# A decoder layer stack on one core: the memory layer's softmax sums move to TensorE, its division to VectorE behind the values, and the normalisations' epsilon to GpSimd

## The reference, cut to what matters

```python
x = x + L0_attn(_layernorm(x))                       # attention
x = x + L0_xattn(_layernorm(x), ctx, mask0)          # linear cross attention
x = x + L0_ffn(_layernorm(x))                        # gated feed-forward
x = x + L1_attn(_layernorm(x))                       # feature attention
x = x + L1_xattn(_layernorm(x), ctx, mask1)          # memory layer
x = x + L1_ffn(_layernorm(x))                        # ternary feed-forward

def _L1_xattn_ref(hidden_states, memory_tokens, memory_mask, norm_w, wq, wk, wv, wo, wg):
    x = rmsnorm(hidden_states, norm_w)
    q, k, v = x @ wq.T, memory_tokens @ wk.T, memory_tokens @ wv.T   # 16 heads of 16
    attn = jnp.einsum('blhd,bmhd->bhlm', q, k) * scale
    attn = jnp.where(memory_mask[:, None, None, :], attn, -jnp.inf)
    attn = jnp.nan_to_num(jax.nn.softmax(attn, axis=-1), nan=0.0)
    out = jnp.einsum('bhlm,bmhd->blhd', attn, v).reshape(B, L, C) @ wo.T
    return jax.nn.sigmoid(x @ wg.T) * out
```

## Time and profile before

| | |
|---|---|
| median of 3 runs | 916.41 us (916.15 to 917.59) |
| the profiled execution | 914.14 us, span 912.3 us |
| mean granted TensorE clock | 0.994 |
| busy: TensorE, VectorE, ScalarE, GpSimd | 93%, 78%, 59%, 41% of the span |

### The profile page before, as it was taken

One profiled execution on the slowest core, in us unless ns is written; L12 is line 12 of the kernel. 1 busy time (PEld: TensorE's weight loads), 2 busy tenths in 40 slices (PEclk: granted clock), 3 DMA queues, 4 the chain that ended last, 5 costly groups with the idle time before them and its releaser, 6 DMA issues. The chain is left out here.

```text
span 912.3 us, 18715 instructions
## 1 busy us (share of the span) xinstructions
PE 848.8 (93%) x6868; PEld 630.7 (69%) x6868; DVE 707.6 (78%) x1749; ACT 539.0 (59%) x1285; POOL 373.0 (41%) x358
## 2 busy tenths in 40 slices
PE   6888998999999999999999998999978889999786
PEld 3555766777777777777777776887855578777554
DVE  5647967887788788877887774997688779886985
ACT  1655576665666566656665655464566864546676
POOL 6014555545555555545554644052242031522410
PEclk9999999999999999999999999999999999999999
DMA  9133131101110111011100000000000010000001
GB/s 279 40 83 93 22 94 36 31 6 35 35 26 8 35 35 35 0 35 35 35 0 11 1 1 2 2 1 1 1 1 1 1 47 1 1 1 1 1 1 47
DMA packets 34723, 25.56 MB, mean 28 GB/s; under 512 B 9492, under 2 KB 31596, under 8 KB 34668
## 3 DMA queue, kind: packets, MB, share of 16 engines
q1 hardware_dynamic: 34380, 24.56, 10.1%
q10 hardware_dynamic: 288, 0.26, 0.1%
HBM read 22.65 MB, written 2.17 MB: 27 GB/s over the span
## 5 line engine op out<-in xcount | busy, mean ns | idle before, releaser
L502 POOL CAST exp_hi<-exp_scores 128x1024 f16<-128x1024 f32 x64 | 67.0, 1047 | 199.4 <-ACT exp_scores L628 199.4
L504 POOL TENSOR_TENSOR exp_lo<-exp_scores,exp_hi 128x1024 f16<-128x1024 f32 x64 | 140.7, 2198 | 5.1
L628 ACT ACTIVATE exp_scores<-banks,exp_bias,unscale 128x256 f32<-128x256 f32 x256 | 141.0, 560 | 2.1
L75 PE MATMUL banks<-value_out_hi,xn_t_hi 128*128 128x256 f16 x512 | 139.6, 273 | 0.8 <-DVE X L961 0.5
L76 PE MATMUL banks<-value_out_lo,xn_t_hi 128*128 128x256 f16 x512 | 139.5, 273 | 0.0
L77 PE MATMUL banks<-value_out_hi,xn_t_lo 128*128 128x256 f16 x512 | 139.5, 273 | 0.0
L1119 PE MATMUL banks<-qk 128*128 128x256 f32 x512 | 121.6, 380 | 8.5 <-ACT exp_scores L628 8.4
L1119 PEld LDWEIGHTS banks<-qk 128*128 128x128 f32 x512 | 96.6, 190 | 29.4 <-issue 8.7
L961 DVE SCALAR_TENSOR_TENSOR X<-banks,colsum,X 128x256 f32<-128x256 f32 x256 | 106.2, 478 | 12.8 <-DVE colsum L952 11.4
L573 ACT ACTIVATE qk<-banks 128x512 f32<-128x512 f32 x128 | 75.8, 601 | 58.9 <-PE banks L77 58.9
L75 PE MATMUL banks<-xn_t_hi,head_weights_hi 128*128 128x512 f16 x256 | 96.9, 378 | 2.4 <-ACT qk L573 1.6
(11 more groups left out here) (254 smaller groups left out, 1962.4 us busy)
## 6 DMA issues: line engine op xcount, KB each, us to landing
head_weights<-in_wqkv_d SPq DMA_DIRECT2D x32, 128.0 KB, 3.8
weight_absmax_rows<-across_partitions SPq DMA_DIRECT2D x15, 256.0 KB, 4.2
X<-in_x_d SPq DMA_DIRECT2D x4, 512.0 KB, 7.6
head_weights<-in_wqkvt_d SPq DMA_DIRECT2D x16, 128.0 KB, 3.5
head_weights<-in_w_o_d SPq DMA_DIRECT2D x16, 128.0 KB, 3.5
out<-X SPq DMA_DIRECT2D x8, 256.0 KB, 2.1
ternary_then_kv_and_rows<-in_c_fc_d SPq DMA_DIRECT2D x1, 1024.0 KB, 5.0
ternary_then_kv_and_rows<-in_c_proj_d SPq DMA_DIRECT2D x1, 1024.0 KB, 8.0
```

The costliest lines, as they stand in the source:

```text
L75: nc.tensor.matmul(out, lhs[0], rhs[0], start=first, stop=False)
L502: nc.gpsimd.tensor_copy(probh[:, s1_.par], prob[:, s1_.par]).then_inc(exph_ready, 1)
L504: nc.gpsimd.tensor_tensor(probl[:, s1_.par], prob[:, s1_.par], probh[:, s1_.par], ALU.subtract).then_inc(expl_ready, 1)
L628: last = nc.scalar.activation(prob[:, s1_.par, t, :], sc_ps[t // ST][:, t % ST, :], ACT.Exp, bias=nbias[:, t:t + 1], scale=unscale[:, s1_. ...
```

## The change

The sums of the exponentials are no longer made by VectorE. TensorE multiplies the transposed, undivided exponentials by the values and, right behind, by `own_ones`: a 128x32 matrix with ones for a head's own 64 rows and zeros elsewhere, so that each sum stands in PSUM beside each of its head's 16 outputs. VectorE takes the reciprocal of those 128x256 sums into `xt` (`rs`) and multiplies output, `anykey` and reciprocal into `ot` (`on`). `sum`, `rd`, `pn` and `ote` go away. `own_ones` is made by three small memsets on GpSimd early in the attention part. The epsilon of every normalisation in the streams moves from VectorE to GpSimd, in front of `pow`. In the ternary layer the factors of 255 are put into the scale beforehand, and `c1` goes away. The list `work` is changed to match, so every queue's order is made anew.

```diff
@@ attention_part, GpSimd, behind rstd_of(3)
+        nc.gpsimd.memset(g.own_ones[:, :, :], 0.0).then_inc(own_ones_set, 1)
+        for a in range(2):
+            pool.wait_ge(own_ones_set, a + 1)
+            nc.gpsimd.memset(g.own_ones[a * M:(a + 1) * M, a, :], 1.0).then_inc(own_ones_set, 1)
+        pool.wait_ge(own_ones_set, 3)
         for a in range(2):
             pool.wait_ge(whi_ready, a + 1)
             weights_lo(0, a)
@@ attention_part, VectorE
-                nc.vector.tensor_scalar(g.tscale255[:, :], g.tscale[:, 1:2], 1.0 / 255.0, None, ALU.mult)
+                nc.vector.tensor_scalar(g.tscale_root[:, :], g.tscale[:, 0:1], float(255.0 ** -0.5), None, ALU.mult)
@@ the list of work
-        return [f"{layer}_stats DVE .66 {after}", f"{layer}_aggr DVE .16", f"{layer}_eps DVE .08", f"{layer}_pow POOL .67",
+        return [f"{layer}_stats DVE .66 {after}", f"{layer}_aggr DVE .24", f"{layer}_eps POOL .2", f"{layer}_pow POOL .67",
-                                         "max DVE 1.13", "sub DVE 1.14", "exp ACT .96", "sum DVE 1.13", "rd DVE .17",
-                                         "pn POOL 1.86", "pt PE 1.02", "pte ACT .92", "o PE .58", "ote ACT .36")]
+                                         "max DVE 1.13", "sub DVE 1.14", "exp ACT .96", "pt PE 1.02", "pte ACT .92",
+                                         "o PE 1.16", "rs DVE .42", "on DVE .42")]
@@ streams_part, GpSimd
+            if part == "eps":
+                ln = norms[layer]
+                pool.wait_ge(ln["mv"], nth_norm(layer, s))
+                inside, eps = (1.0 + 1e-6, LN_EPS * 1e-6) if layer == "mem" else (1.0, LN_EPS)
+                nc.gpsimd.tensor_scalar(rstd[s][:, :], mv[s][:, :, 1], inside, eps, ALU.mult, ALU.add).then_inc(ln["veps"], 1)
-            elif part == "pn":
-                t = tile_of(layer)
-                pool.wait_ge(mem_rden[t], n[s])
-                nc.gpsimd.tensor_tensor(by_head(s), by_head(s), den[s][:, t, :].unsqueeze(2).broadcast_to([P, XH, M]),
-                                        ALU.mult).then_inc(mem_pn[t], 1)
@@ streams_part, ScalarE
-            elif layer in ("mem0", "mem1") and part == "ote":
-                t = tile_of(layer)
-                act.wait_ge(mem_o_full[t], n[s])
-                nc.scalar.activation(ot[s][:, :, t * P:(t + 1) * P], PA[s][:, 0:KT * P].rearrange("p (k n) -> p k n", k=KT),
-                                     ACT.Copy, scale=g.anykey[:, s:s + 1]).then_inc(mem_o[t], 1)
@@ streams_part, VectorE
-            elif part == "sum":
-                dve.wait_ge(mem_exp[t], n[s])
-                nc.vector.tensor_reduce(den[s][:, t, :], by_head(s), AX.X, ALU.add).then_inc(mem_sum[t], 1)
-            elif part == "rd":
-                dve.wait_ge(mem_sum[t], n[s])
-                nc.vector.reciprocal(den[s][:, t, :], den[s][:, t, :]).then_inc(mem_rden[t], 1)
+            elif part == "rs":
+                dve.wait_ge(mem_o_full[t], n[s])
+                nc.vector.reciprocal(xt[s][:, t, :], PA[s][:, KT * P:2 * KT * P]).then_inc(mem_rden[t], 1)
+            elif part == "on":
+                dve.wait_ge(mem_rden[t], n[s])
+                by_tile = lambda ap: ap.rearrange("p (k n) -> p k n", k=KT)
+                nc.vector.scalar_tensor_tensor(out=ot[s][:, :, t * P:(t + 1) * P], in0=by_tile(PA[s][:, 0:KT * P]),
+                                               scalar=g.anykey[:, s:s + 1], in1=by_tile(xt[s][:, t, :]), op0=ALU.mult,
+                                               op1=ALU.mult).then_inc(mem_o[t], 1)
@@ streams_part, VectorE, ternary layer
-            elif part == "c1":
-                dve.wait_ge(ter_step[s], s // STREAMS * 3 * ST + 3 * t + 2)
-                nc.vector.tensor_scalar(small[s][:, 7:8], small[s][:, 6:7], float(np.sqrt(255.0)), None,
-                                        ALU.mult).then_inc(ter_scale[t], 1)
@@ streams_part, TensorE
             elif part == "pt":
-                pe.wait_ge(mem_pn[t], n[s])
+                pe.wait_ge(mem_exp[t], n[s])
@@ in piece o
                 for j in range(XH // 2):
                     rows = slice(j % 4 * 2 * XD, (j % 4 + 1) * 2 * XD)
-                    last = nc.tensor.matmul(PA[s][rows, j // 4 * P:(j // 4 + 1) * P],
-                                            g.v1[:, s, j].rearrange("p a e -> p (a e)"), pt[s][:, j * P:(j + 1) * P],
-                                            start=True, stop=True)
+                    for at, values in ((j // 4, g.v1[:, s, j]), (KT + j // 4, g.own_ones[:, :, :])):
+                        last = nc.tensor.matmul(PA[s][rows, at * P:(at + 1) * P], values.rearrange("p a e -> p (a e)"),
+                                                pt[s][:, j * P:(j + 1) * P], start=True, stop=True)
```

More of the change, by code:

```diff
@@ L208, in attention_part @@
     x_loaded = [sem(f"x_loaded{p}") for p in range(NP)]
+    own_ones_set = sem("own_ones_set")
     consts_ready, ident_clear, ident_ready = sem("consts_ready"), sem("ident_clear"), sem("ident_ready")
@@ L1308, in norm_sems @@
     def norm_sems(name):
-        return {k: sem(f"{name}_{k}") for k in ("veps", "rstd", "xn", "xt_full", "xt_ready", "added")}
+        return {k: sem(f"{name}_{k}") for k in ("mv", "veps", "rstd", "xn", "xt_full", "xt_ready", "added")}
     lin, ffn, fat, mem, ter = (norm_sems(k) for k in ("lin", "ffn", "fat", "mem", "ter"))
@@ L1331, in streams_part @@
     two = lambda k: [sem(f"mem_{k}{t}") for t in range(ST)]
-    mem_s_full, mem_max, mem_sub, mem_exp, mem_sum, mem_rden, mem_pn = (
-        two(k) for k in ("s_full", "max", "sub", "exp", "sum", "rden", "pn"))
+    mem_s_full, mem_max, mem_sub, mem_exp, mem_rden = (
+        two(k) for k in ("s_full", "max", "sub", "exp", "rden"))
     mem_pt_full, mem_pt, mem_o_full, mem_o = (two(k) for k in ("pt_full", "pt", "o_full", "o"))
@@ L1341, in streams_part @@
     stored = sem("stored")
-    NORM = ["stats", "aggr", "eps", "sh", "xn", "lo"]
+    NORM = ["stats", "aggr", "sh", "xn", "lo"]
     ROWS_BY_SCALAR = ("mem", "ter")
@@ L1381, in streams_part @@
         work += [f"ter{t}_{w}" for w in ("h PE 1.74" + (" ter0_nte ter0_add" if t else ""), "max DVE 1.13", "m0 DVE .12",
-                                         f"relu ACT 1.0 ter{t}_max", f"c0 DVE .24 ter{t}_m0", "c1 DVE .08",
-                                         f"sq ACT 1.04 ter{t}_relu ter{t}_c1", "n DVE .6", "nt PE .45", "nte ACT .91",
+                                         f"relu ACT 1.0 ter{t}_max", f"c0 DVE .24 ter{t}_m0",
+                                         f"sq ACT 1.04 ter{t}_relu ter{t}_c0", "n DVE .6", "nt PE .45", "nte ACT .91",
                                          "out PE .9", "add DVE .4")]
@@ L1412, in stage @@
         def stage(s, name, layer, part):
-            if part == "pow":
+            if part == "eps":
[3 more added lines that the diff above has]
+                nc.gpsimd.tensor_scalar(rstd[s][:, :], mv[s][:, :, 1], inside, eps, ALU.mult, ALU.add).then_inc(ln["veps"], 1)
+            elif part == "pow":
                 ln = norms[layer]
@@ L1558, in norm_stage @@
             elif part == "aggr":
-                dve.wait_ge(norm_step[s], s // STREAMS * 2 * len(norms) + 2 * nth - 1)
+                dve.wait_ge(norm_step[s], s // STREAMS * len(norms) + nth)
                 dve.sem_inc(turn, 1)
@@ L1562, in norm_stage @@
                     last = nc.vector.bn_aggr(mv[s][:, t, :], st6[s][:, t, :])
[L1563 to L1572, removed]
+                last.then_inc(ln["mv"], 1)
             elif part == "sh":
@@ L1700, in ternary_stage @@
                 dve.wait_ge(ter_max[t], n[s])
-                nc.vector.tensor_scalar(small[s][:, 5:6], small[s][:, 4:5], g.tscale[:, 0:1], float(np.sqrt(1e-5)),
-                                        ALU.mult, ALU.max).then_inc(ter_step[s], 1)
+                nc.vector.tensor_scalar(small[s][:, 5:6], small[s][:, 4:5], g.tscale_root[:, 0:1],
+                                        float(np.sqrt(1e-5 / 255.0)), ALU.mult, ALU.max).then_inc(ter_step[s], 1)
             elif part == "c0":
-                dve.wait_ge(ter_step[s], s // STREAMS * 3 * ST + 3 * t + 1)
-                nc.vector.reciprocal(small[s][:, 6:7], small[s][:, 5:6]).then_inc(ter_step[s], 1)
+                dve.wait_ge(ter_step[s], s // STREAMS * 2 * ST + 2 * t + 1)
+                nc.vector.reciprocal(small[s][:, 7:8], small[s][:, 5:6]).then_inc(ter_scale[t], 1)
                 nc.vector.tensor_scalar(small[s][:, 9 + t:10 + t], small[s][:, 5:6], small[s][:, 5:6],
-                                        g.tscale255[:, 0:1], ALU.mult, ALU.mult).then_inc(ter_step[s], 1)
-            elif part == "c1":
-                dve.wait_ge(ter_step[s], s // STREAMS * 3 * ST + 3 * t + 2)
-                nc.vector.tensor_scalar(small[s][:, 7:8], small[s][:, 6:7], float(np.sqrt(255.0)), None,
-                                        ALU.mult).then_inc(ter_scale[t], 1)
+                                        g.tscale[:, 1:2], ALU.mult, ALU.mult).then_inc(ter_step[s], 1)
```

(5 more changed lines are left out.)

## The result

The changed kernel takes 932.96 us (median of 4 runs, 930.82 to 933.67), the kernel before 917.0: 1.017 times as long, 95% interval 1.0152 to 1.0189. It is slower, as forecast, by 16 us where 8 were forecast. The profiled execution had 933.7 us, span 931.9. It is the longest of its four, and that of the kernel before (914.1 us, span 912.3) is shorter than all four behind its median: the two profiles differ by 19.6 us, the medians by 16.0. Ratios leave out single executions in a slower state (one each of e2, e11c, e12 and, beside e5 to e7, of the kernel before).

A forecast was written before the change was run, and what follows sets the result against it. VectorE's queue bounds the memory stage's middle, latency with TensorE its ends. Terms: +7.6 VectorE, -1.0 other epsilons and c1, +0.5 hand-overs, +0.9 TensorE, +8.0 in all: 924.4 us median, range 916.0 to 934.

The forecast's parts named there:

- The step that failed: Memory stage: VectorE's +5.3 us a round, 1.5 absorbed by slack and idle time, leaving +3.8 a round, +7.6 for both.
- the stretch that it had in mind: Memory layer from first maximum to last gated addition; some 4 us longer each round, with VectorE above 90%.
- Rival B: Memory stage: order planned with rs at 0.42 makes TensorE wait at second tiles' scores; +15, 931 us; chance 0.24.
- The epsilons: Streams' normalisations: moving epsilons off VectorE, including a long one of 0.95 us, takes 1.1 us of VectorE a round.
- The small sums: Streams: -1.0 us for c1 and epsilons outside the memory stage, +0.5 for hand-overs of epsilon to GpSimd.
- The passes of own_ones: Memory layer, TensorE: 8 more matmuls a tile, +0.5 us each tile, mostly in gaps; +0.9 over both rounds.
- C: End of the memory stage: latency decides, saving 2.4 us a round, -5 in all, 911 to 912 us; chance 0.12.
- D: Memory stage: exit saving and VectorE's growth cancel, 913 to 918.2 us, middle 916; chance 0.11.
- rival E: Memory layer: reciprocal streams at one element a ns, 0.48 us; -8 us in all, 906; chance 0.04.
- the exit gap: Last tile of the memory round: 4.8 us between exponential and transposes, saved except 0.1, against 2.3 paid.

The follow-up runs named there:

- e2: Changed kernel with a plain copy of the sums in place of their reciprocal, same queue orders: 912.86 us, ratio 0.9959 to the kernel before.
- e11c: Changed kernel with VectorE's sums and 128x16 reciprocal, spread by GpSimd, transposed by TensorE, no ones products; heads' reciprocals mixed up: 913.0 us, ratio 0.9967.
- e12: Changed kernel with 128x16 reciprocal spread by GpSimd and transposed by TensorE, no ones products, heads in the right order: 913.06 us, ratio 0.9965.
- e5: Kernel before with epsilon on GpSimd and c1 gone, memory layer as before, queues kept in the old order by hand: 915.72 us, ratio 0.9994.
- e7: Changed kernel with ScalarE copying values and sums out of PSUM, rs and on working in SBUF, order planned anew: 926.51 us, ratio 1.011.
- e8c: Changed kernel with the reciprocal over 128 of the 256 columns only, same queue orders: 917.33 us, ratio 1.0012 to the kernel before.
- e1: Changed kernel with measured lengths in the list of work (rs 1.69, on 0.4, o 1.05), orders made from them: 931.75 us, ratio 1.015.
- e10c: Changed kernel with ScalarE copying values and sums out of PSUM, and the list of work at measured lengths: 924.49 us, ratio 1.0092.
- e6: The whole change put by hand into the order planned for the kernel before: 947.18 us, ratio 1.0333 to the kernel before.
- e3: Kernel before with epsilon on GpSimd and c1 gone, memory layer as before, order planned anew: 922.89 us, ratio 1.0062.
- e9c: Changed kernel with a copy in place of the reciprocal and without the products with own_ones: 910.88 us, ratio 0.9928 to the kernel before.

## Why the prediction was right and wrong

**The sign and the cause were right.** The reciprocal's length makes the loss: without it the same structure in the same order takes 912.9 us (e2), with it 933.0. The idea of what bounds the stage was wrong by the prediction's own sign, see the step below.

**The prices were right.** 1.75 us against 1.77 for the reciprocal; the Trainium skill's repeat count ("VectorE: DVE Perf Modes", section "First, the fixed hardware budget"), from which the prediction's estimate was 2.13 us, is too dear here: the measured 1.75 us decides, and from 128 to 256 columns the runs have 800 ns for 128, or 6.25 ns each. The product, the epsilon, the memsets of own_ones (0.13 and 2 x 0.14 us) were as costed. So was TensorE's piece o: the first passes of a tile start at 670.15 and the next tile's transposes at 671.20, 1.05 us against the forecast 1.1. Four passes in a row for one column group did not block the next (2.9 us was the price if they had). VectorE's busy time over the whole span grew by 7.1 us, where some 9 were expected.

```profile
670.15 0.45 PE L1866 MATMUL banks<-mid_stream,v 128*32 128x128 f32 x8
...
671.20 1.09 PE L1858 MATMUL banks<-ident,big_stream 128*128 128x128 f32 x8
```

**The step that failed** is in the sum: "I take 1.5 of it as absorbed, +3.8 a round, +7.6 for both". The stage grew by 7.6 to 7.7 us a round, twice that. VectorE's work is not the reason: it grew by 4.3 to 4.4 where 5.3 were in the sum. The absorption is. VectorE's idle time was to take 1.5 of the growth; instead it grew by 3.3 us itself. The idea behind the step was that one queue sets the middle of the stage and slack takes some of its growth. The prediction had named a sign against it: "If VectorE's share in the stage stays under 85%, my bound was wrong". The share is 77% here; from the first maximum on, the stretch that it had in mind, 84% in the second round and 82% in the first, where above 90% was expected. (That stretch itself grew by 2.3 to 2.4 us, not 4, since the new order puts the first maximum 5 us later; in e2, with the same late start, the whole stage is shorter than before.) e5 speaks against the bound too. And e2, e8c and the changed kernel show a price that rises: about half of one to one, then 1.1 to 1.2 to one, with no absorption left at the reciprocal's full length.

**Rival B's mechanism is in it, but not as B had it.** I gave B 0.24 and 931 us; the time came out at 933. The nearness is in part luck. B's sign was new waits of 2 us before the scores of second tiles; these are 1.2 us at most, 4.0 in all against 2.9 before. The waits of 3.3 and 2.7 us stand elsewhere, before the output product and before the transposes. The first is the last tile's own latency on the way out, the second comes from VectorE's queue. What e7 gained by taking the scores' wait away can't be told from what its new order gained. The other half of B, that the order planned with 0.42 does the harm, holds for 1 to 2 us at most by the medians (e1, e10c), and the old order is 14 us worse (e6).

**The clock was in no rival.** In the windows above 3.25 us of standing are followed by an output product at half clock, 1.8 us more; the long transposes of the second round (870.98, 1.64 us against 1.09) follow a wait of 2.68 us in the same manner. The changed kernel's two stages have 12.3 us at half clock, those of the kernel before 3.4, e2's and e8c's none. The 8.9 us more are at most 4.5 us of lost TensorE time, an estimate; by the executions at like clocks some 3 of the 16 us go with it.

How the 8 missing us divide among idle queues, order and clock stays open.

**The epsilons.** -1.1 us of VectorE a round was about right as busy time (1.5 with the stage's short ones, e5) and wrong as time: e5 gains nothing. The small sums (-1.0, +0.5) can't be told from zero. That a new order alone can cost 7 us (e3) is a case that the prediction didn't have.

**The passes of own_ones**: +0.9 was forecast; 2 us were measured where TensorE's queue is the fuller one (e9c against e2), with intervals that overlap.

**Rivals C, D and E** are out: the exit gap did go (the transposes follow the exponential at once), and the stage grew nevertheless; rival E's 0.48 us would have been a gain, as e2's 0.42 shows.

**What stays open.** In the profiles 2.5 us of the 19.6 between the two spans lie before the streams (first feed-forward addition at 612.31 instead of 609.80 us), 15.3 in the two stages, 1.8 elsewhere. The memsets don't explain the 2.5, for GpSimd is idle for 3.03 us behind them; e5, which has no memsets, is 1.4 us late there. Much of it seems to be the execution and not the kernel: the event lies between 609.8 and 616.5 us in the profiles of this case, at 610.8 in e10c, which has the memsets, and latest in e12, with 17.1 us at half clock before it; the kernel before has 6.8 there, the changed kernel 10.2. How e6's 14 us arise in detail was not followed.

## What to carry to other kernels

Price a reciprocal by its columns (here 6.3 ns each): divide where the tensor is narrowest, and spread the result with engines that have time. A piece that stands between a PSUM bank and its reuse can cost twice, once in its own queue and once in TensorE's; letting a free engine copy the bank out first is worth a try (5.5 to 6.5 us here, together with a new order). Where queue orders are planned, compare a moved piece in the old order as well as in the new, and don't credit an edit with what its new order did: the new order alone was worth +7 us for one change and -14 for another.

## What the runs showed that was not expected

Lengthening one piece in steps of 0.5 and 0.8 us cost 0.5 and then 1.1 to 1.2 times its added time: the price of a queue is no constant. At the far end VectorE was busy for 77% of the stage and TensorE for 87%, and both were idle longer than in e8c (15.8 us against 14.3, 8.7 against 2.8). And a short stand of TensorE can halve the clock behind it, but need not: of the changed kernel's four stands of 2.7 to 3.3 us in the memory stages three were followed by 3.4 to 6.8 us at 0.50, the fourth by none. The kernel before had 3.4 us at 0.50 in its first round behind waits of 1.4 and 1.8 us, and none behind the same waits in its second. A profile of one round is thus not enough to price such a wait.
